# The soft MoE's norms and transposes as pieces of the first attention program, with the RMS factor taken from the layer norm's variance

## The reference

```
x = _layernorm(x + _L0_xattn_ref(x, ctx_768, ...))         # the last norm of the first attention program
x = _layernorm(x + _L0_ffn_ref(x, ...))

def rmsnorm(x, gamma):
    n = jnp.linalg.norm(x, axis=-1, keepdims=True)
    return x / jnp.maximum(n, 1e-12) * SCALE * gamma       # SCALE = 16, the root of 256
xn = rmsnorm(x, norm_gamma)                                 # 2048 rows of 256
sn = rmsnorm(slot_embeds, slot_norm_gamma)                  # 8 experts x 128 slots, no input but a weight
logits = jnp.einsum('bnd,esd->bnes', xn, sn)
```

## Time and profile before

| | us |
|---|---|
| median of 3 runs | 2955.36 (2954.71 to 2956.67) |
| the profiled execution | 2954.8 |
| its span, first to last instruction | 2953.1 |
| PE busy in the span | 2536.9 (86%) |
| DVE, ACT, POOL busy | 1502.1, 1340.6, 456.4 |
| mean granted TensorE clock | 0.933 of full speed |

### The profile page before, as it was taken

One profiled execution on the slowest core, in us unless ns is written; L12 is line 12 of the kernel. 1 busy time (PEld: TensorE's weight loads), 2 busy tenths in 40 slices (PEclk: granted clock), 3 DMA queues, 4 the chain that ended last, 5 costly groups with the idle time before them and its releaser, 6 DMA issues. The chain is left out here.

```text
span 2953.1 us, 47417 instructions
## 1 busy us (share of the span) xinstructions
PE 2536.9 (86%) x15793; PEld 1452.1 (49%) x15794; DVE 1502.1 (51%) x4196; ACT 1340.6 (45%) x2886; POOL 456.4 (15%) x719
## 2 busy tenths in 40 slices
PE   6999999999549889997889899898977995399991
PEld 3555544444224456675555544343434654267761
DVE  2555877888044500024544588777735663222224
ACT  3655467766444422111445457565664552022220
POOL 4233211110200000000122212212023001400004
PEclk8999999999969999998899999999998996599996
DMA  6544533321000022114633433232322325501113
GB/s 207 165 138 139 132 87 93 75 59 43 6 12 1 1 91 91 60 47 151 182 105 122 133 97 90 58 92 63 78 68 75 108 66 189 176 31 32 32 32 91
DMA packets 153825, 259.89 MB, mean 88 GB/s; under 512 B 22712, under 2 KB 96704, under 8 KB 149440
## 3 DMA queue, kind: packets, MB, share of 16 engines
q1 hardware_dynamic: 150544, 248.81, 28.8%
q0 software_dynamic: 3072, 8.39, 0.9%
HBM read 180.71 MB, written 81.53 MB: 89 GB/s over the span
## 5 line engine op out<-in xcount | busy, mean ns | idle before, releaser
L1357 ACT ACTIVATE second_p<-psum 128x512 f32<-128x512 f32 (+3 forms) x1024 | 461.9, 522 | 278.9 <-PE psum L1223 275.4
L1357 ACT ACTIVATE first_p<-psum 128x512 f32<-128x512 f32 (+3 forms) x768 | 365.8, 548 | 171.5 <-PE psum L1223 168.5
L1431 DVE TENSOR_REDUCE second_max_parts<-psum 128x1 f32<-128x512 f32 x512 | 321.5, 682 | 67.7 <-PE psum L1200 66.5
L1431 DVE TENSOR_REDUCE first_max_parts<-psum 128x1 f32<-128x512 f32 x512 | 322.2, 682 | 57.4 <-PE psum L1200 55.6
L1427 DVE CUSTOM_DVE_ANT_0 second_masked<-psum,mask_qk 128x384 f32<-128x384 f32 (+3 forms) x512 | 229.2, 488 | 194.5 <-PE psum L1200 169.8
L1213 PE MATMUL psum<-second_q,second_k 64*128 64x512 f32 (+3 forms) x1024 | 226.1, 437 | 42.8 <-DVE second_max_parts L1431 27.1
L1235 PE MATMUL psum<-second_p,second_v_aug 128*32 128x512 f32 (+3 forms) x2048 | 238.6, 538 | 8.4 <-ACT second_p L1357 8.1
L1200 PE MATMUL psum<-second_k,second_q 64*128 64x512 f32 (+3 forms) x1024 | 201.9, 391 | 27.9 <-DMA second_k<-a_k_parts 15.6
L1213 PEld LDWEIGHTS psum<-second_q,second_k 64*128 64x128 f32 x1024 | 98.1, 187 | 231.3 <-issue 84.0
L1223 PE MATMUL psum<-second_shift_T,choose 64*128 64x512 f32 (+3 forms) x1024 | 197.6, 381 | 0.0
L1235 PE MATMUL psum<-first_p,first_v_aug 128*32 128x512 f32 (+3 forms) x1536 | 184.1, 551 | 11.6 <-ACT first_p L1357 11.6
(11 more groups left out here) (317 smaller groups left out, 3800.4 us busy)
## 6 DMA issues: line engine op xcount, KB each, us to landing
first_k<-c_k_parts SPq DMA_DIRECT2D x64, 256.0 KB, 4.7
second_q<-a_q_parts SPq DMA_DIRECT2D x128, 128.0 KB, 2.9
second_k<-a_k_parts SPq DMA_DIRECT2D x128, 128.0 KB, 2.9
second_k<-c_k_parts SPq DMA_DIRECT2D x64, 256.0 KB, 4.6
first_q<-a_q_parts SPq DMA_DIRECT2D x64, 128.0 KB, 2.9
first_k<-a_k_parts SPq DMA_DIRECT2D x64, 128.0 KB, 2.9
c_k_parts<-first_held SPq DMA_DIRECT2D x16, 512.0 KB, 3.1
first_q<-c_q_parts SPq DMA_DIRECT2D x64, 128.0 KB, 4.5
```

What stands on the lines that cost most here:

```text
L1357: evacuated(act.activation(probs[tile % 2][:, 2 * h + p, q0:SEQ], bank[:, q0:SEQ], ACT.Exp, scale=scale), event)
L1431: evacuated(v.reduce_max(max_parts[n % 2][:, h, p, qt, k0 // BANK:k0 // BANK + 1], bank[:, 0:width], axis=AX_X), event)
```

## The change

- The slot embeddings and both gains are fetched at the start of the first attention program, into the buffer that later holds the normed rows (`soft["rows"]`).
- `slot_pieces` (statistics, root, scaling, four turns of four transposes each) are put behind the other pieces of group 19. The mean square is taken as mean squared plus variance.
- For each cross-attention slot `output_pieces` gains "rms_rows" (DVE) and two "rms_turn". The factor of the RMS norm is computed on POOL from the layer norm's variance: var / (var + eps) is the mean square after the layer norm. `roots_with_scale` takes two roots at once and then three more instructions: 19 steps where `root_of` has 15.
- In slot 7 the four multiplications of the layer norm go from POOL to DVE (`applied_late`).
- The context tiles share memory with the buffers of the transposed slots and rows. `rms_turn` has a cost of 450 in `COST`, the other new pieces 300.
- `soft_moe` starts with `stage_soft_routes`: three stages are gone.

```diff
+def slot_pieces():
+    return [("slot_stats", 0, 0), ("slot_root", 0, 0), ("slot_rows", 0, 0)] + [("slot_turn", 0, u) for u in range(EXPERTS // QT * DK)]
@@ output_pieces
+    if layer.scaled:
+        pieces += [("rms_rows", slot, 0)] + [("rms_turn", slot, k) for k in range(DK)]
-COST = {"oturn": 450, "xturn": 450, "oproj": 1750, "split": 1750, "value": 1750}
+COST = {"rms_turn": 450, "oturn": 450, "xturn": 450, "oproj": 1750, "split": 1750, "value": 1750}
@@ stage_attentions, sync, ahead of the list
+                if soft:
+                    embeds = soft["rows"][:, 0:EXPERTS, :]
+                    sp.dma_start(embeds, a["L0_ffn_slot_embeds"].rearrange("e s d -> s e d")).then_inc(soft_in, 16)
+                    sp.dma_start(slot_gain[:, :], a["L0_ffn_slot_norm_gamma"].partition_broadcast(P)).then_inc(soft_in, 16)
+                    sp.dma_start(rms_gain[:, :], a["L0_ffn_norm_gamma"].partition_broadcast(P)).then_inc(soft_in, 16)
@@ gpsimd
+                def roots_with_scale(slot):
+                    variance, place = mean_var[:, :, 1], scale_at[slot]
+                    step(pool.tensor_scalar(near[:, 0, 0:QT], variance, LN_EPS, None, ALU.add))
+                    step(pool.tensor_scalar(near[:, 0, QT:2 * QT], variance, ROW_LEAST, None, ALU.max))
+                    newton(two_roots[:, :], 2 * QT)
+                    step(pool.tensor_copy(rstd[:, :], two_roots[:, 0:QT]))
+                    wait_for(pool, spread, QT * place)
+                    step(pool.tensor_tensor(near[:, 2, 0:QT], two_roots[:, QT:2 * QT], near[:, 0, 0:QT], ALU.mult))
+                    pool.tensor_tensor(rms_scale[:, :], near[:, 2, 0:QT], rstd[:, :], ALU.mult).then_inc(scaled, 1)
@@ apply
+                    if slots[slot].scaled:
+                        roots_with_scale(slot)
+                    else:
+                        root_of(mean_var[:, :, 1], rstd)
+                    if slot == applied_late:
+                        return
@@ tensor
+                def slot_turn(event):
+                    u = event[2]
+                    pe.wait_ge(slot_ready, EXPERTS)
...
+                def rms_turn(event):
+                    _, slot, k = event
+                    pe.wait_ge(spread, QT * (scale_at[slot] + 1))
...
@@ vector
+                def measure_slots():
+                    v.wait_ge(soft_in, 48)
+                    for e in range(EXPERTS):
+                        v.bn_stats(slot_stats[:, e, :], soft["rows"][:, e, :]).then_inc(slot_done, 1)
...
+                def scale_slots():
+                    v.wait_ge(slot_inverted, 1)
+                    for e in range(EXPERTS):
+                        v.scalar_tensor_tensor(soft["rows"][:, e, :], soft["rows"][:, e, :], slot_root[:, e:e + 1], slot_gain[:, :],
+                                               ALU.mult, ALU.mult).then_inc(slot_ready, 1)
+                def rms_rows(slot):
+                    place, b = scale_at[slot], slot % BATCH
+                    v.wait_ge(scaled, place + 1)
+                    if slot == applied_late:
+                        for t in range(QT):
+                            v.tensor_scalar(x_of(slot)[:, t, :], x_of(slot)[:, t, :], mean_var[:, t, 0:1], rstd[:, t:t + 1],
+                                            ALU.subtract, ALU.mult).then_inc(applied, 1)
+                    if place == 0:
+                        wait_full(v, ("slot_turn", 0, EXPERTS // QT * DK - 1))
+                    v.wait_ge(applied, QT * (norm_at[slot] + 1))
+                    for t in range(QT):
+                        v.scalar_tensor_tensor(soft["rows"][:, b * QT + t, :], x_of(slot)[:, t, :], rms_scale[:, t:t + 1],
+                                               rms_gain[:, :], ALU.mult, ALU.mult).then_inc(spread, 1)
@@ soft_moe
-        with nc.sbuf_tensor("soft_slot_T", [P, DK, ES], F32) as slot_T:
-            with nc.sbuf_tensor("soft_embeds", [P, EXPERTS, D], F32) as embeds:
-                stage_fetch(c, "soft_embeds_in", [(embeds[:, :, :], a["L0_ffn_slot_embeds"].rearrange("e s d -> s e d"))])
-                stage_norm(c, "slot", embeds, EXPERTS, rms=a["L0_ffn_slot_norm_gamma"], dstT=slot_T)
-            stage_between(c, f"{name}_in", rms=a["L0_ffn_norm_gamma"], rows_to=c.rows)
-            stage_soft_routes(c, c.rows, slot_T, slots_T, combine)
+        stage_soft_routes(c, c.rows, slot_T, slots_T, combine)
@@ build
+        pieces[GROUPS * BATCH + GROUPS - 1] += slot_pieces()
```

111 lines of the change are left out of this document (88 added, 23 removed).

## The result

The changed kernel takes 2970.7 us (median of 5 runs, 2968.5 to 2972.0) beside 2955.4 us for the kernel before (2954.5 to 2956.9): ratio 1.005, 95% interval 1.0036 to 1.0065. It is slower, by 15 us where 9 were forecast.

A forecast was written before the change was run, and what follows sets the result against it. PE was taken to bound the cross-attention groups, while a chain of other engines leaves it nearly idle at the seam; -48.0 + 43.0 + 14.0 = +9.0 us gave 2964 us, with 8 in 10 between 2951 and 2975.

The forecast's parts named there:

- The sum: Whole kernel: seam -48.0, groups 21, 25, 29 +43.0, group 19 +14.0, together +9.0 us.
- Seam, -48.0: Between attention and soft MoE: routes start at 811.75 in place of 859.73, minus 48.0 us, bounds 46 and 50.
- Groups 21, 25, 29, +43.0: Cross-attention groups: PE idle 11.7 us, lower clock 1.6, transposes 1.04, so 14.3 each, plus 43.0 for three.
- The 8.53 us seen in the second program: PE's measured idle time at the second program's like wait, taken as lower bound for the 11.7 us stop.
- The split of the other 2.6 us: Per group 21, 25, 29 beside the idle time: 1.6 us for the lower clock, 1.04 for eight more transposes.
- Group 19, +14.0: Slots' work, once: PE idle 10.3 us, clock 1.6, sixteen transposes 2.1, plus 14.0 us.
- The start, 0 with a bound of 1.8: Program start: transfers issued behind the first layer's weights cost 0, at most 1.8 us.
- the prediction's own sign of being wrong: At the start: PE's wait for its first weights ending later than 16 us would show the prediction wrong.
- Rival 2: Cross-attention groups: PE doesn't stop, only transposes (5.2 us) remain; 2912 us, chance 0.11.
- Rivals 1: Four stops in groups 19, 21, 25, 29 no longer than 8.53 us, sides cancel: -2.3, 2953 us; chance 0.15.
- rival 3: Groups and start: stops cost as the longest (14.05 us), clock 2.2 each, start 1.8; +24, 2979 us; chance 0.12.

The follow-up runs named there:

- experiment 6: Changed kernel with ten more small multiplications in POOL's chain of each of slots 4 to 7: 2978.5 us, ratio 1.0082 to the kernel before.
- 7: Changed kernel with the layer norm's last four multiplications of slots 4 to 6 on DVE instead of POOL: 2955.5 us, ratio 1.0005 to the kernel before.
- experiment 5: Changed kernel with only the transposes of slots 4 to 6 moved to the next group, scaling left in place: 2954.2 us, ratio 1.0004 to the kernel before.
- 1: Changed kernel with the rows' DVE scaling and transposes of slots 4 to 6 moved to groups 22, 26, 30: 2925.5 us, ratio 0.9902 to the kernel before.
- experiment 12: Changed kernel with 13 unused products keeping PE busy before the rows' first transposes of slots 4 to 6: 2964.2 us, ratio 1.0025 to the kernel before.
- Experiment 2: Changed kernel with the slots' scaling and transposes moved from group 19 to group 20: 2961.6 us, ratio 1.0028 to the kernel before.
- experiment 3: Changed kernel with the transfers of slot embeddings and two gains issued before group 5's load, not at the start: 2971.8 us, ratio 1.0062 to the kernel before.

## Why the prediction was right, and what was off

- **The sum.** The three named terms came to -47.8 + 43.3 + 13.5 = +9.0, as forecast. What was counted as nothing came to some +4.3 in the profiled execution: +4.0 by group 17, +1.7 in the last projection and -1.4 behind the seam. The first two are told below; the third was not traced.
- **Seam, -48.0.** Measured -47.8. The routes start 15.0 us after POOL's first step, as worked out (14.8); the clearing of the stage behind ACT's last copy takes 3.76 us, 3.45 predicted. The six new semaphores cost 0.12 us each by this, not 0.07.
- **Groups 21, 25, 29, +43.0.** Measured +15.4, +14.2 and +14.8, less 0.55 each in groups 22 and 26, which the sum didn't have: +43.3. The stop was 11.70, 11.66 and 11.66 us, forecast 11.7, and the experiments show its parts: POOL's chain (6, 7), DVE's queue (5) and, with both consumers moved, its end (1). The 8.53 us seen in the second program, where PE's queue is free, has its like in experiment 5: 9.6 us, with POOL's chain four steps longer.
- **The split of the other 2.6 us was off.** The lower clock costs 2.7, 1.6 and 2.5 us (experiment 12) in place of 1.6, and the transposes leave 0.9 in place of 1.04. The 1.6 came from a stop behind which the clock rose 3.7 us after PE resumed. Here it rose after 6.1, 3.5 and 5.5 us; the row of group 21 stands above (mean 0.59 from 560, so up at 560.8), and those of the other two, where PE resumed at 673.33 and 790.80, are

```profile
676.00:677.00 1.00, 1.00 (x10) 0.15 (x8) 0.94 (x2) 0.78 (x2) 0.00 (x0) 0.56 0.00 0
...
796.00:797.00 1.00, 1.00 (x7) 0.57 (x7) 0.00 (x0) 0.71 (x2) 0.00 (x0) 0.83 0.00 0
```

Each comes to 0.44 us lost for a microsecond at the lower clock (2.67 of 6.1, 1.55 of 3.5, 2.46 of 5.5), and the old row to 0.43. So the rate was right, and the time at the lower clock, which differs between three stops of the same code, was taken from one stop. The Trainium skill's TensorE: Matmul & The Clock Gate, Part 1, puts such a ramp under 1% of a kernel's span; that agrees, since three of them are 6.7 us or 0.2%, and this is nearly half of the 15 us in question.
- **Group 19, +14.0.** Measured +13.5; stop 9.90 (10.3 worked out). Experiment 2 adds what the sum did not name: with that stop gone, groups 19 and 20 are still 8.3 us above the kernel before, of which 5.4 are PE's two waits behind the lumps on DVE.
- **The start, 0 with a bound of 1.8: the mis-sized term.** Group 17 ended 4.0 us later. The first weights came 1.1 us later, at 16.89, so that the prediction's own sign of being wrong, a wait past 16, came true. The clock rose later in group 0 (mean from 64 to 68 us 0.50, before 0.81), which ended 2.2 us later, beyond the bound; experiment 3 shows that the transfers do this. The argument that what is issued behind the awaited transfers is free failed: with them the DMA engines carry more during the wait (0.82 busy for 0.57), and the awaited ones land later. Another 1.7 us is the clock in group 5 (below), which is not the change's.
- **Last projection, not predicted, +1.7.** In the changed kernel's window 849.00 to 853.00 the clock is 0.74, the first half of the projection takes PE 3.58 us where it took 1.96, and the last drain stands 12.3 us ahead of POOL's start in place of 10.6. The other traces settle that this isn't the change's: in seven of the thirteen executions that have it, the distance is 10.6 us again at a clock of 1.00; in four it is 12.2 to 12.3 at 0.86, in one 13.1 at 0.74, in one 14.6 at 0.65. All have the same code there. So of the 13.4 us, 3.4 are falls of the clock, here and in group 5, that other executions of the same code do not have: a single pair of traces can't tell them from the change.
- **Rival 2** had the right condition, the distance between aggregate and scaling, and nearly the right time: with that distance made, the kernel takes 2925.5, and 2915.1 with the slots moved too, against 2912 for no stop at all. Rivals 1 (2953) and 3 (2979) are refuted by the length of the stops; but in two smaller terms rival 3 was nearer than the forecast, the clock (2.2 us a stop; 2.7, 1.6 and 2.5 measured) and the start (1.8; 2.2).

The rule of the Trainium skill's Perfetto Trace Analysis (section "Per-instruction lifecycle: what the profiler-reported window actually captures"), to go by starts on GpSimd, agrees with experiment 6: ten steps whose bars are 0.2 us lengthen the stop by 3.05.

## What to carry to other kernels

Before work is moved into the slack of a busy program, count the steps of the plan between the start of a slow chain and each queue that consumes it, and compare them with the chain's length: one step of 2.9 us before a chain of 10.3 cost 15 us a group, five cost at most 1.5. Then move all its consumers, on every engine: DVE's, left behind, still stopped PE for 9.6 us. Averages of busy time hide lumps: here 2.7 us of DVE work in one piece stopped PE, and pieces of 0.75 and 0.88 us didn't. Ask of every piece, a POOL chain or a transfer too, what stands behind it in its own queue.

## What the runs showed of the hardware

A stop of about a microsecond may or may not cost the clock. Between groups 4 and 5 PE waits 1.3 us in both kernels for ACT's copy of the transposed outputs (`first_oT`), which the output projection reads: the profile names no releaser, but by the code `output_project` waits for that copy, and the product starts 0.1 us behind its end. The changed kernel, then the kernel before:

```profile
153.97 0.65 ACT L1449 ACTIVATE first_oT<-psum 128x512 f32<-128x512 f32 x1
154.72 3.61 PE L1330 MATMUL psum<-first_a_wo,first_oT 128*128 128x256 f32 x8 [1.28 <-issue]
```

```profile
152.52 1.97 PE L1277 MATMUL psum<-first_a_wo,first_oT 128*128 128x256 f32 x8 [1.27 <-issue]
```

Windows of 1 us, in the same order:

```profile
154.00:155.00 1.00, 0.28 (x1) 0.31 (x2) 0.07 (x1) 0.62 (x2) 0.00 (x0) 0.82 0.99 373
155.00:156.00 1.00, 1.00 (x3) 0.82 (x3) 0.00 (x0) 0.00 (x0) 0.00 (x0) 0.50 0.99 273
...
158.00:159.00 1.00, 1.00 (x12) 0.69 (x10) 0.64 (x1) 0.00 (x0) 0.00 (x0) 0.98 0.57 197
```

```profile
152.00:153.00 1.00, 0.48 (x2) 0.49 (x3) 0.00 (x0) 0.42 (x1) 0.00 (x0) 1.00 1.06 377
153.00:154.00 1.00, 1.00 (x6) 0.87 (x6) 0.00 (x0) 0.00 (x0) 0.00 (x0) 1.00 1.05 270
```

The one is at the 1.2 GHz level for some 3.4 us and its projection loses 1.6 us (3.61 for 1.97), the other stays at 2.4 GHz. Group 5 took 18.6 us in the changed kernel and in experiments 1 to 3, and 16.9 in the other nine and before, with the same instructions. Such steps of 1.5 to 1.7 us at other groups make part of the scatter; what decides whether one comes was not found. The Trainium skill's TensorE: Matmul & The Clock Gate, Part 1, says that the length of the ramp varies from run to run. The rows agree: the same code stayed at the lower level for 6.1, 3.5 and 5.5 us behind its three long stops; and behind the short one it fell to it in one execution and not in another.
